# Expert phase of a gated attention and mixture-of-experts block: token tiles turned by a DMA transpose, gathers issued ahead of adds, up to three adds in flight, weight loads in four pieces

## What is computed

```python
logits = x @ gate_w.T
probs = softmax(logits)
top_w, top_i = top_k(probs, 2)
top_w = top_w / sum(top_w)
for e in range(12):
    h = silu(x @ w1[e].T) * (x @ w3[e].T)
    out = out + h @ w2[e].T * cw[:, e:e + 1]
x = x + tanh(g_ffn[0]) * out
```

## Time and profile before

| | us |
|---|---|
| median of 3 runs | 837.55 (837.42 to 838.53) |
| the profiled execution, span from its first to its last instruction | 830.0 |
| what a run's time has around such a span (837.55 - 830.0) | 7.55 |
| PE matmul busy | 630.5 (76%) |
| DVE busy | 419.5 (51%) |
| ACT busy | 332.3 (40%) |
| POOL busy | 243.7 (29%) |
| granted TensorE clock, mean | 0.919 |

### The profile page before, as it was taken

How to read it: one execution, slowest core, us unless ns; L and a number is a source line. 1 busy time by engine, 2 the same in 40 slices (tenths; PEclk the granted TensorE clock), 3 DMA queues, 4 the chain that set the end, 5 groups by cost and what they waited for, 6 DMA issues and landing times.

```text
span 830.0 us, 13872 instructions
## 1 busy us (share of the span) xinstructions
PE 630.5 (76%) x4169; PEld 270.9 (33%) x4170; DVE 419.5 (51%) x763; ACT 332.3 (40%) x394; POOL 243.7 (29%) x186
## 2 busy tenths in 40 slices
PE   3438669888896988989767140599989898999993
PEld 1202213123131221313212010465545454666661
DVE  4777556566574766657556536553323332333330
ACT  5125656565675665656744000022222221222221
POOL 5212123151331414223012111333333333344432
PEclk9999979899999999989978555699999999999998
DMA  4677885958779495876957387155666666645452
GB/s 153 177 209 208 202 251 151 268 163 188 222 192 265 139 259 174 165 250 182 240 166 220 94 274 293 54 125 156 177 177 177 177 174 171 172 90 97 80 90 39
DMA packets 75371, 146.52 MB, mean 177 GB/s; under 512 B 10757, under 2 KB 36870, under 8 KB 73798
## 3 DMA queue, kind: packets, MB, share of 16 engines
q1 hardware_dynamic: 43664, 68.18, 30.6%
q10 hardware_dynamic: 22038, 55.35, 21.8%
q0 software_dynamic: 9632, 22.55, 14.7%
HBM read 87.85 MB, written 53.74 MB: 171 GB/s over the span
## 4 chain that ended last, share of the span: by engine, by line
PE 32%; DMA 29%; issue 18%; POOL 7%; DVE 7%; SPq 4%; ACT 2%; ACTq 0%; DVEq 0%; POOLq 0%
DMA out<-yo,slot_out 10%; PE S L1286 9%; DMA residual<-x 6%; PE O L1307 6%; PE O L1151 5%; PE MA L1187 4%; DMA xg<-tokens_normed,slot_tok 4%; DMA K<-k_parts 3%; PE S L1112 3%; PE MC L1187 2%; SPq L463 2%; PE S L1274 1%; DMA W<-weight_parts 1%; DMA q_parts<-qs 1%; POOL cs L536 1%
## 5 line engine op out<-in xcount | busy, mean ns | idle before, releaser
L655 ACT ACTIVATE prob<-S 128x1024 f32<-128x1024 f32 x256 | 246.1, 1023 | 183.5 <-PE S L1112 144.7
L1286 PE MATMUL S<-W,xT 128*128 x1032 | 149.1, 301 | 1.2 <-DVE xT L1060 1.2
L1151 PE MATMUL O<-prob,V 128*32 128x512 f32 x1024 | 149.3, 646 | 0.0
L1112 PE MATMUL S<-Q,K 49*128 49x512 f16 x512 | 92.5, 411 | 63.4 <-DMA K<-k_parts 41.6
L593 POOL DMA_INDIRECT out<-yo,slot_out x43 | 69.2, 1609 | 171.1 <-DMA out<-yo,slot_out 84.0
L1286 PEld LDWEIGHTS S<-W,xT 128*128 128x128 f16 x1032 | 99.3, 98 | 39.0 <-issue 1.3
L1307 PE MATMUL O<-W,hT 128*128 (+1 forms) x344 | 91.9, 387 | 0.9 <-DVE hT L1080 0.9
L1068 DVE SCALAR_TENSOR_TENSOR hh<-S,act 128x320 f32<-128x320 f32 x43 | 21.1, 492 | 123.0 <-PE S L1286 123.0
L1112 PEld LDWEIGHTS S<-Q,K 49*128 49x128 f16 x512 | 20.3, 95 | 192.7 <-ACT prob L655 134.5
L762 DVE SCALAR_TENSOR_TENSOR wp<-wf,wp 128x1024 f16<-128x1024 f32 x48 | 69.6, 1451 | 1.7
L536 POOL TENSOR_TENSOR cs<-ctx,cs 128x1024 f16<-128x1024 f32 x8 | 17.0, 2126 | 151.5 <-DVE cs L823 151.5
(11 more groups left out here) (149 smaller groups left out, 647.7 us busy)
## 6 DMA issues: line engine op xcount, KB each, us to landing
wf<-wall ACTq DMA_DIRECT2D x48, 512.0 KB, 7.0
weight_parts<-wp ACTq DMA_DIRECT2D x48, 512.0 KB, 5.0
W<-weight_parts SPq DMA_DIRECT2D x10, 2048.0 KB, 9.1
Q<-q_parts SPq DMA_DIRECT2D x48, 128.0 KB, 8.2
K<-k_parts SPq DMA_DIRECT2D x48, 128.0 KB, 8.5
ctx<-ctx_in SPq DMA_DIRECT2D x8, 512.0 KB, 12.6
residual<-x SPq DMA_DIRECT2D x8, 512.0 KB, 14.3
k_parts<-ks SPq DMA_DIRECT2D x8, 512.0 KB, 2.8
```

The lines of the kernel that those rows point to most:

```text
L655: act.activation(prob[:, u % RING, :], S[u % 2][:, :], ACT.Exp, scale=SCALE).then_inc(g.exp, 1)
L1112: last = pe.matmul(S[u % 2][:, s * T:(s + 1) * T], K[par][r0:r0 + PARTS * DK + 1, 2 * g4 + n, st * P:(st + 1) * P], Q[par][r0:r0 + PARTS * ...
L1151: last = pe.matmul(O[g4 % 2][2 * DK * j:2 * DK * (j + 1), :], V[par][:, st, GH * g4 + j, :], prob[:, u % RING, (j % 2) * T:(j % 2 + 1) * T ...
L1286: last = pe.matmul(ps, xT[par][:, xp * TT + k, :], W[:, bass.ds(off + (w * WCOL + (2 * k + n) * F), F)], start=(k == 0 and (xp, w) == (0, 0)),
```

## The change

- `turn_x` leaves the PE and `x_out` leaves the DVE. ACT issues one DMA transpose for each tile, `xg` to `xT`, 128 x 1024 fp16 in SBUF to 128 x 8 x 128 in SBUF. It issues that of tile j + 2 (AHEAD) at the start of its step j, ahead of `gate_tile`. `xT` has four buffers instead of two.
- A gather into `xg` now waits for the DMA transpose of the tile four before (`s_xT`), and POOL issues gather j + 4 ahead of add j - 2 (LAG), instead of behind add j.
- Up to three adds (DEEP) are in flight. Add j waits for add j - 3 always, and for adds j - 1 and j - 2 only where the tile belongs to another expert than that one, or is unused. A small table `turns` says so: six DVE instructions after the routing make it. From tile 7 on POOL reads it with a register load for each add.
- `yo` becomes free by `s_landed`, which POOL raises when it has seen an add landed, instead of by the DMA's own semaphore.
- Each weight load is four DMAs of 512 KB (4 KB for each partition) in a row, and the numbers in `table` are four times as large.

The core of the diff:

```diff
+    LAG = 2
+    DEEP = 3
+    AHEAD = 2
+    PIECES = 4
...
-        xT = [sb(f"xT{i}", [P, 2 * TT, P], F16) for i in range(2)]
+        xT = [sb(f"xt_sb{i}", [P, 2 * TT, P], F16) for i in range(TR)]
...
+        def load_expert(eng, e):
+            flat = w_dram[e].rearrange("p h n -> p (h n)")
+            step = 2 * WCOL // PIECES
+            for n in range(PIECES):
+                at = (e % EB) * 2 * WCOL + n * step
+                eng.dma_start(W[:, at:at + step], flat[:, n * step:(n + 1) * step]).then_inc(s_wr, 16)
...
-                sp.wait_ge(s_wr, 16 * e)
-                sp.dma_start(W[:, (e % EB) * 2 * WCOL:(e % EB + 1) * 2 * WCOL],
-                             w_dram[e].rearrange("p h n -> p (h n)")).then_inc(s_wr, 16)
+                sp.wait_ge(s_wr, 16 * PIECES * e)
+                load_expert(sp, e)
...
             def gather(j):
                 if j >= TR:
-                    pool.wait_ge(s_xt, j - TR + 1)
+                    pool.wait_ge(s_xT[j % TR], 16 * (j // TR))
...
+            def add(j):
+                if j >= DEEP:
+                    pool.wait_ge(s_add[(j - DEEP) % TR], 16 * ((j - DEEP) // TR + 1))
+                    pool.sem_inc(s_landed, 1)
+                if 1 <= j < TR + DEEP - 1:
+                    pool.wait_ge(s_yo, j + 1)
+                    pool.wait_ge(s_add[(j - 1) % TR], 16 * ((j - 1) // TR + 1))
+                elif j >= 1:
+                    turn = pool.value_load(turns[0:1, j:j + 1], min_val=0, max_val=3)
+                    behind1 = pool.to_reg((turn & 1) * 16 + 16 * ((j - 1) // TR))
+                    behind2 = pool.to_reg((turn & 2) * 8 + 16 * ((j - 2) // TR))
+                    pool.wait_ge(s_yo, j + 1)
+                    pool.wait_ge(s_add[(j - 1) % TR], behind1)
+                    pool.wait_ge(s_add[(j - 2) % TR], behind2)
+                else:
+                    pool.wait_ge(s_yo, 1)
+                pool.indirect_dma_start(out=out[:, :],
+                                        out_offset=bass.IndirectOffsetOnAxis(ap=slot_out[:, j:j + 1], axis=0),
+                                        in_=yo[j % TR][:, :], in_offset=None, compute_op=ALU.add)\
+                    .then_inc(s_add[j % TR], 16)
...
-            for j in range(TILES):
-                pool.wait_ge(s_yo, j + 1)
-                if j >= 1:
-                    pool.wait_ge(s_add, 16 * j)
-                pool.indirect_dma_start(out=out[:, :],
...
+            pool.wait_ge(s_turns, 1)
+            for j in range(TILES + LAG):
                 if j + TR < TILES:
                     gather(j + TR)
-            pool.wait_ge(s_add, 16 * TILES)
+                if j >= LAG:
+                    add(j - LAG)
...
             def weigh(act, j, n):
                 wait(act, s_y, j, 1, 2)
-                if n >= TR:
-                    wait(act, s_add, j, 16, 16 - 16 * TR)
+                wait(act, s_landed, j, 1, 1)
...
+            def turn_x(act, j, n):
+                q = At(j.i, j.mul // TR, j.add // TR)
+                if n >= TR:
+                    wait(act, s_h, j, 1, 1 - TR, s_spare)
+                wait(act, s_xg[n % TR], q, 16, 16, s_spare)
+                act.dma_start_transpose(out=xT[n % TR][:, :, :], in_=xg[n % TR][:, :]).then_inc(s_xT[n % TR], 16)
...
             def step(act, j, n):
+                if n < TILES - AHEAD:
+                    turn_x(act, At(j.i, j.mul, j.add + AHEAD), n + AHEAD)
                 gate_tile(act, j, n)
                 hi_part(act, j, n)
...
             act.wait_ge(s_tok, 3)
+            for n in range(AHEAD):
+                turn_x(act, At(None, 0, n), n)
...
-            def x_out(dve, j, n):
-                wait(dve, s_xt, j, 1, 1)
-                if n >= 2:
-                    wait(dve, s_h, j, 1, -1)
-                dve.tensor_copy(xT[n % 2][:, :, :], xt_ps.rearrange("p (k n) -> p k n", n=P)).then_inc(s_xT, 1)
...
-            def turn_x(j, n):
-                pe.wait_ge(s_xg[n % TR], At(j.i, j.mul // TR, j.add // TR).value(16, 16))
-                wait(pe, s_xT, j, 1)
-                for k in range(2 * TT):
-                    last = pe.transpose(xt_ps[:, k * P:(k + 1) * P], xg[n % TR][:, k * P:(k + 1) * P], ident16[:, :])
-                last.then_inc(s_xt, 1)
...
-                wait(pe, s_xT, j, 1, 1)
+                wait(pe, s_xT[n % TR], At(j.i, j.mul // TR, j.add // TR), 16, 16, s_table)
                 if n >= 1:
                     turn_h(j.before(1), (n - 1) % 2)
-                hidden(j, n % 2, off)
-                if n < TILES - 1:
-                    turn_x(At(j.i, j.mul, j.add + 1), n + 1)
+                hidden(j, n % TR, off)
                 if n >= 1:
                     down(j.before(1), (n - 1) % 2, off_before)
```

More of the change, by code:

```diff
@@ L255, in flamingo_kernel @@
         table = sb("table", [P, TILES + NE], U16)
+        et_c = sb("et_c", [P, TILES])
+        turned = sb("turned", [P, 2, TILES])
+        unused = sb("unused", [P, TILES])
+        turns = sb("turns", [P, TILES], U16)
         xg = [sb(f"xg{i}", [P, 2 * T], F16) for i in range(TR)]
-        xT = [sb(f"xT{i}", [P, 2 * TT, P], F16) for i in range(2)]
+        xT = [sb(f"xt_sb{i}", [P, 2 * TT, P], F16) for i in range(TR)]
         act1 = [sb(f"act1_{i}", [P, F]) for i in range(2)]
@@ L359, in flamingo_kernel @@
         s_xg = [sem(f"s_xg{i}") for i in range(TR)]
-        s_xt = sem("s_xt")
-        s_xT = sem("s_xT")
+        s_xT = [sem(f"s_xT{i}") for i in range(TR)]
         s_h1 = sem("s_h1")
@@ L381, in tiles @@
                 step(eng, At(None, 0, n), n)
-        s_add = sem("s_add")
+        def load_expert(eng, e):
[4 more added lines that the diff above has]
+                eng.dma_start(W[:, at:at + step], flat[:, n * step:(n + 1) * step]).then_inc(s_wr, 16)
+        s_add = [sem(f"s_add{i}") for i in range(TR)]
+        s_turns = sem("s_turns")
+        s_landed = sem("s_landed")
         s_stored = sem("s_stored")
@@ L672, in _ @@
                 if e >= 1:
-                    act.wait_ge(s_wr, 16 * e)
-                act.dma_start(W[:, e * 2 * WCOL:(e + 1) * 2 * WCOL], w_dram[e].rearrange("p h n -> p (h n)"))\
-                    .then_inc(s_wr, 16)
+                    act.wait_ge(s_wr, 16 * PIECES * e)
+                load_expert(act, e)
             act.wait_ge(s_wexp, 1)
@@ L1052, in _ @@
                                      op0=ALU.mult, op1=ALU.add).then_inc(s_tok, 1)
-            def x_out(dve, j, n):
-                wait(dve, s_xt, j, 1, 1)
-                if n >= 2:
-                    wait(dve, s_h, j, 1, -1)
-                dve.tensor_copy(xT[n % 2][:, :, :], xt_ps.rearrange("p (k n) -> p k n", n=P)).then_inc(s_xT, 1)
+            last = done(dve.tensor_scalar(unused[:, :], et_f[:, :], NE - 0.5, None, ALU.is_gt))
+            for n in range(2):
+                last = done(dve.tensor_tensor(turned[:, n, 2:TILES], et_f[:, 2:TILES], et_f[:, 1 - n:TILES - 1 - n],
+                                              ALU.is_gt))
+            then(last)
+            for n in range(2):
+                last = done(dve.tensor_tensor(turned[:, n, 2:TILES], turned[:, n, 2:TILES], unused[:, 2:TILES], ALU.max))
+            then(last)
+            dve.scalar_tensor_tensor(out=turns[:, 2:TILES], in0=turned[:, 1, 2:TILES], scalar=2.0,
+                                     in1=turned[:, 0, 2:TILES], op0=ALU.mult, op1=ALU.add).then_inc(s_turns, 1)
             def step(dve, j, n):
@@ L1264, in _, with hidden @@
             pe.sem_inc(s_y, 1)
-            def turn_x(j, n):
-                pe.wait_ge(s_xg[n % TR], At(j.i, j.mul // TR, j.add // TR).value(16, 16))
-                wait(pe, s_xT, j, 1)
-                for k in range(2 * TT):
-                    last = pe.transpose(xt_ps[:, k * P:(k + 1) * P], xg[n % TR][:, k * P:(k + 1) * P], ident16[:, :])
-                last.then_inc(s_xt, 1)
             def weights_of(j):
-                landed = pe.value_load(table[0:1, bass.ds(j.value(), 1)], min_val=16, max_val=16 * NE)
-                return landed, ((landed - 16) & (16 * (EB - 1))) * (2 * WCOL // 16)
-            def hidden(j, par, off):
+                one = 16 * PIECES
+                landed = pe.value_load(table[0:1, bass.ds(j.value(), 1)], min_val=one, max_val=one * NE)
+                return landed, ((landed - one) & (one * (EB - 1))) * (2 * WCOL // one)
+            def hidden(j, n_, off):
                 for n, (ps, full) in enumerate(((h1_ps, s_h1), (h3_ps, s_h))):
@@ L1285, in hidden @@
                         for xp, w in ((0, 0), (0, 1), (1, 0)):
-                            last = pe.matmul(ps, xT[par][:, xp * TT + k, :],
+                            last = pe.matmul(ps, xT[n_][:, xp * TT + k, :],
                                              W[:, bass.ds(off + (w * WCOL + (2 * k + n) * F), F)],
```

16 lines of the change are left out of this document (6 added, 10 removed).

## The result

The change made the kernel slower: **867.0 us** median of 4 runs (865.88 to 869.99) against 837.93 (837.42 to 838.53) of the kernel before, measured beside it. The ratio is 1.0383, 95% interval 1.0334 to 1.0433. The forecast was 797, range 788 to 825. The profiled execution took 867.27 us with a span of 865.5.

What follows compares the result with a forecast made beforehand. The PE was taken to bound stretches without weight loads, with hold-ups by late adds beside loads. 837.55 - 18.0 (PE transposes) - 27.0 (hold-ups) + 2.6 (start) + 2.0 (PE issue) = 797.1 us, range 788 to 825.

Steps and rivals of the forecast that it cites:

- The hold-ups: PE waits beside weight loads: reordered gathers, overlapping adds and finer loads would remove all 27.0 us (bounds 0 to 27.0).
- The room: Time ACT's transpose issue could take per tile at no cost: 3.2 us from the start of `weigh`, 2.5 from its end.
- The four pieces: Weight loads in 4 KB pieces should interleave more finely with 2 KB gather and add rows; shares the 27.0 us gain.
- B: Rival, chance 0.15: DMA engines fill up beside loads, 6.17 us a tile over some 24 tiles, 17 us more: 814.
- A: Slower rival, chance 0.12: the transpose sets each tile's period, 910 us; an ACT issue over 4.2 us would do the same.
- C: Rival, chance 0.06: the PE's queue is the real bound at 5.92 us, removing its transposes frees nothing: 815.
- D: Rival, chance 0.05: the hold-ups stay, since the loads' bytes delay everything whatever the packets or order: 824.
- E: Rival, chance 0.04: POOL's small instructions take 3.5 us, not under 2.6, so 6.4 us a tile for 36 tiles: 829.
- Transposes off the PE: Eight matmuls a tile leave the PE's path, 0.44 us for each of 41 periods: 18.0 us saved.
- The 2.0 us put down for PE issue: Added idle on the PE's own queue ahead of `turn_h`, which has two register loads there; bounds 0 to 6.0 us.
- The start: First `hidden` waits for a transpose landing in 4.4 us instead of 1.8: 2.6 us lost (bounds 1.6 to 6.4).
- The margin around the span: The 7.55 us between profiled span and median time, kept unchanged; the forecast span was 789.6 us.

## Why the prediction was wrong, point by point

**The hold-ups, 27.0 us taken as gone: the step that failed.** With the gathers ahead of the adds and the adds overlapping, every tile takes 5.92 us and no hold-up is left (803.9 us); so far the step was right. What failed is the overlap behind it: the transpose, "issued two steps, 11 us, before its `hidden`", with a landing put at 4.4 us (8.2 at most) and so "hidden by the 11 us". I took landing and issue of the transpose from rows without a load beside it. As such they were good enough: 4.4 us forecast, 3.0 to 3.1 measured alone; an issue of about 1 us forecast, 1.25 measured. At the eight loads the transpose that the PE waited for landed in 14.5 to 21.1 us. So the 27.0 us did not go to zero but to 71.9. The row that should have warned me is the earlier trace rows: an add in flight took 4.72 us alone and 9.02 beside a load. I used it for the old hold-ups and not for the new transfer, which has eight packets (256 B) for each row (2 KB) of a gather of the same bytes. ACT's issue took up to 10.1 us, far over its room, but in the change that lay in the shadow of the landing. The room itself, 2.5 to 3.2 us, is borne out by the run with one DMA a load: 2.4 to 2.9.

**The four pieces.** "A load in 4 KB pieces should interleave more finely" was not tried by itself; with 1 KB pieces the kernel before did lose 16 of its 27 us (814.3). Where gathers ahead and adds in flight had already removed the hold-ups, the four pieces brought nothing (807.8 with four, 803.9 with one). Beside transposes they are 45 us worse than one DMA (867.0 to 822.3).

**The rivals.** B had the right place and the right sign, waits for `xt_sb` only beside loads with a share near 1, but the wrong size. It put a transpose at 1.42 us of DMA time a tile. Without load bytes that was about right: 1.6, by the estimate above. But adding it to a loaded tile gave 6.17 us, and the change has 8.3. Of A, which had all of the 0.12 for slower, neither way came true. Its own mechanism, each transpose slower than a tile, did not: alone they land in 3.0 to 3.1 us. Its last sentence, that an ACT issue of over 4.2 us would do the same, wanted one in every tile; there were nine, of 5.4 to 10.1 us, none of them what ended a stop. By the Trainium skill's 1309 ns a block ("VectorE: DVE Perf Modes", section The three transpose paths) eight blocks one after another would take 10.5 us, an estimate. Here one DMA of eight blocks landed in 3.0 to 3.1 us, so the blocks do not add up in that way. The Trainium skill's page that I set against it, "Advanced Engine Details and Errata", section X-Bar Transpose (TRN2), which says that transposing DMAs are as fast as others, agrees with the transposes by themselves: 3.0 to 3.1 us, the gather's 256 KB 4.4. Beside a load they took up to 21.1 us, and gathers up to 15.6. C was half right: undisturbed tiles came down from 5.92 to 5.72 only. D and E did not happen.

**Transposes off the PE, 18.0 us.** The period was to be 5.48 and is 5.72. The 0.44 us are gone, but 0.19 came back between `down` and `turn_h` (2.14, not 1.95) and 0.05 between `turn_h` and `hidden` (0.32, not 0.27). I had read the parts from the last tile, whose waits are against constants; the change's own last period, 5.53, is shorter too. In the loop the chain through ACT and DVE ends at 820.79 and `down` has had its 1.95 us at 820.85, as forecast, but `turn_h` starts at 821.04. Part of this delay belongs to the PE's own instructions, since moving two of them gets 5.60. That is 41 x 0.24 = 9.8 us, so the transposes' going was worth 8.2 us (41 x 0.20), not 18.0. The 2.0 us put down for PE issue were meant for this and too few.

**The start, 2.6 us lost.** From the first gather's issue to `hidden` it is 530.70 - 521.4 = 9.3 us, where before it was 5.4: 3.9 lost. The transposes:

```profile
525.14 4.75 ACTq L748 DMA_TRANSPOSE xt_sb<-xg  x3
...
530.71 5.01 PE L1325 MATMUL S<-W,xt_sb 128*128 x24 [7.57 <-DMA xt_sb<-xg]
```

From the first one's issue to `hidden` it is 5.6 us, not 4.4, with three of them issued in a row.

**The margin around the span.** I kept 7.55 us between span and median. A run of the change has 1.8 us around its span (867.27 - 865.5). The rest was probably that the profiled execution of before was quicker than its median: the attention half differs by some microseconds from one execution to the next. The sum itself, taken against the median, was not touched by this. The upper end of the forecast's own range, given as 806, comes out of its terms as 804.9; nothing rests on that.

Put together: with no load bytes in the way the change gives 800.8 us, 3.7 over the forecast, but that is closer than the terms were. The 42 periods took 243.6 us, where the sum has 277.0 - 18.0 - 27.0 + 2.0 = 234.0. The miss beyond that is the pair of transposes and loads.

## What to carry to other kernels

A price read where a transfer is alone does not hold where another stream shares the DMA engines: before a DMA is put on a compute engine's queue, look for the slowest transfer of the trace beside the largest load, and ask what stands behind the issue on that engine. Undo the parts of a bundled change one by one: here issuing gathers ahead and letting adds overlap was together worth 4% (0.9599), and the DMA transposes beside loads in four pieces turned it into a loss. When a stop shows a blocked engine, follow the chain that ended last before blaming it: the block may lie in the shadow of another transfer. And read a period from a tile inside the loop, not from the last one.

## What the runs showed of the hardware that I had not expected

- A DMA transpose of 128 x 1024 fp16 within SBUF costs ACT's queue 1.25 us to issue and lands in 3.0 to 3.1 us (least and median) when nothing large is beside it.
- Such transposes beside a weight load in four 4 KB-packet DMAs need more packet time than the two apart, some 8.3 us a tile against 6.2 by estimate: from 640 to 680 us a share of 1.04 at 168 GB/s, against 0.77 at 214 GB/s without them. In other cuts they do not: sixteen DMAs of 1 KB packets have 1.12 at 256 GB/s.
- Issuing is not free of the transfers: 1.25 us becomes 10.1 beside a load and 26.2 in the worst of the cuts, and half as many packets for each transpose keep it at 1.2 to 2.2. In one run the first 2.4 to 2.9 us of an issue cost nothing and the rest was paid in full.
- The same 2 MB to the same place, cut in nine ways, made a kernel of 808.5 to 1060.8 us. Whole rows for 8 or 32 partitions in each DMA were worst, and with 8 a load took 23.5 us and more with no transpose near.
